# A macaron block on one core: turning h and x in the last stage with VectorE and DMAs

## The chip, the cores and the metric

The kernel runs on one core of a Trainium2 chip. The time is the device time of one execution in microseconds, the median of several runs. Engines are named as in the profile: PE (TensorE matmul) with PEld (its weight load), DVE (VectorE), ACT (ScalarE), POOL (GpSimd) and SP (SyncE), whose queue only issues DMAs here.

## The reference

x is 8192 tokens of 512 features. The block is a half-weighted small FFN, an attention block with a delta rule and a GELU MLP, and the same small FFN again:

```python
x = x + 0.5 * ffn(layernorm(x))
r = layernorm(x)
h = rmsnorm(r, ln1); r = r + gdn_attention(h)
h = rmsnorm(r, ln2); r = r + gelu(h @ w1 + b1) @ w2 + b2
x = x + r
x = x + 0.5 * ffn(layernorm(x))

# ffn(x): s = x @ Win + bin (64 columns); 16 relu terms for each column,
#         weighted by W2 and summed, + b2; then @ Wout + bout
```

Only the last stage is touched: the MLP (512 to 2048 to 512), the residuals x + r, and the second small FFN.

## The kernel before

The program has three stages behind each other. The first (to about 937 us) does the first FFN and the projections, the second (to about 1700 us) the delta rule, the third, "dense", the rest, in NT = 16 tiles of TOK = 512 tokens. A tile is Z[t % 2], 128 partitions (tokens) by 4 blocks by 512 features. Each engine has its own function with its own hand-written order (pe_dense, act_dense, dve_dense, pool_dense, sp_dense); they meet only at semaphores, and each engine works strictly in its order.

A tile has NM = 16 units m, one for each 128 of the 2048 hidden columns. In a unit PE does up(t, m), 12 matmuls (w1 against h, both split into a high and a low part, three products, lines 236 to 238 of the helper `product`), then down(t, m - 1), another 12 against w2. ACT makes gelu(t, m) (L1824) and its high part gh (L1828), DVE the low part glo (L1950). After unit 15 comes down(t, 15), and with it the tile ends on PE.

The matmuls need h with features on the partitions, while Z has tokens there. For the next tile, ACT squares z(t+1) in units 12 and 13 (L1809, sums in ss3), DVE and POOL make the inverse root (L1933, L2087), DVE scales z into the buffer H (scale_h in unit 14, L1938), and PE transposes H in 16 blocks of 128x128 into two PSUM banks (turn_h, L1683): 8 after up(t, 15) and 8 after down(t, 14). From the banks ACT writes the high part of h with the factor ln2 (h_turned, L1815) and DVE the low part (h_low, L1942).

The second small FFN of tile t - 1 runs in the units of tile t. DVE makes the statistics of the finished Z (L1960), ACT normalises it into H in units 1 and 2 (L1836), PE transposes H in units 3 and 4 (turn_x, L1692), 8 blocks each, ACT copies the banks to x2T, called xT3 in the code (x_turned, L1846). PE multiplies with Win in unit 5 (hidden, L1700), ACT and DVE do eight relus and sums in units 5 to 7 (L1854, L1980, L1984), PE multiplies with Wout in units 8 and 9 (ffn_out, L1709), DVE adds (L1990). POOL adds x1 and b2 to Z of tile t (add_x1, L2096 and L2098) once x1 has landed in H, and bout to that of tile t - 1 (L2118).

H is thus used in turn for the squares' unused output, scaled h, normalised x and x1. SP issues, for each t: load_x1(t) into H once both turns are done (L1646), the store of tile t - 1 (L1650), the load of z(t+1) into Z (L1640). The last tile's FFN is done in two halves behind the loop (turn_half and others, L1748 and L1756). In tile 0 the pieces of w2 are still being loaded and split; xT3 and Z[1] are their staging buffers, so z(1) is loaded after the last split.

## Time and profile before

| | |
|---|---|
| time, median of 3 runs | 3290.64 us (3287.76 to 3292.36) |
| the profiled execution: its time | 3292.13 us |
| its span, first to last instruction | 3290.3 us |
| mean granted clock of PE | 0.98 |
| busy: PE, PEld, DVE, ACT, POOL | 3131.8, 2549.8, 1827.6, 1405.5, 1226.3 us |
| DMA | 355.09 MB, mean 108 GB/s; HBM read 183.93 MB, written 153.09 MB |
| last stage: up and down matmuls | 6144 of 128x512, each recorded at about 0.39 us and overlapping its neighbours, so that starts are 0.23 us apart |

A line of the timeline has the start in microseconds from the span's start, the duration, the engine, the line of the code, the operation with output and input, and in brackets the idle time of the engine before it and who ended it. A matmul's recorded duration includes its way through the array, so the distance between starts is the better measure of what it costs. The chain of waits is the work that ended last, followed back from the end.

### The profile page before, as it was taken

To read this page: it belongs to the slowest core of one execution; us is meant where nothing else is said; L and a number is where in the kernel's file an instruction comes from. 1 tells how busy PE (TensorE), PEld (TensorE's weight loads), DVE (VectorE), ACT (ScalarE), POOL (GpSimd) and SP (SyncE) were. 2 spreads that over 40 slices of the span, in tenths; PEclk is the share of its full clock that TensorE was granted. 3 is DMA by queue.
4 is the path that set the end of the run, shared out by engine and by line. 5 is a ranking of instruction groups with operands and counts; after the bars stand their busy time and mean duration, and the time that the engine had idled before them with its cause. 6 is when DMAs were issued, how large, how long until landed. Compare 5 with 4: busy or idle time off the path is not lost.

```text
span 3290.3 us, 148463 instructions
## 1 busy us (share of the span) xinstructions
PE 3131.8 (95%) x68236; PEld 2549.8 (77%) x68236; DVE 1827.6 (56%) x2949; ACT 1405.5 (43%) x3166; POOL 1226.3 (37%) x1225
## 2 busy tenths in 40 slices
PE   6999999999948999999999999999999999999998
PEld 4777676767737888989888777888777888777886
DVE  6787878787748888888323333323333323333333
ACT  5544444444314554554543333433333433333433
POOL 1436565656526778766202122212122211122221
PEclk8999999999959999999999999999999999999999
DMA  3455555555466777766750110010111010111010
GB/s 114 142 148 168 155 168 143 179 142 165 137 187 188 225 223 225 216 211 199 211 155 29 39 39 26 27 39 26 39 39 35 17 39 26 39 39 39 14 39 26
DMA packets 393669, 355.09 MB, mean 108 GB/s; under 512 B 59472, under 2 KB 321744, under 8 KB 393424
## 3 DMA queue, kind: packets, MB, share of 16 engines
q1 hardware_dynamic: 391200, 350.88, 35.0%
q8 instruction: 158, 2.59, 0.3%
q10 hardware_dynamic: 2224, 0.90, 0.2%
q14 instruction: 87, 0.71, 0.1%
HBM read 183.93 MB, written 153.09 MB: 102 GB/s over the span
## 4 chain that ended last, share of the span: by engine, by line
PE 61%; DVE 7%; issue 2%; ACT 1%; DMA 0%; SPq 0%; DVEq 0%; ACTq 0%
PE bank L238 14%; PE bank L236 14%; PE bank L237 14%; PE bank L1237 8%; PE bank L1322 6%; DVE tmp L1487 2%; DVE sysf L1491 2%; PE bank L1700 2%; PE bank L1709 2%; PE bank L1692 1%; PE bank L1683 1%; DVE zb L1510 1%; DVE oT_lo L1504 1%; DVE xt L1475 1%; ACT oT_hi L1406 0%
## 5 line engine op out<-in xcount | busy, mean ns | idle before, releaser
L1950 DVE TENSOR_TENSOR glo<-gl,gh 128x512 fp32r<-128x512 f32 x256 | 196.0, 766 | 823.3 <-ACT gh L1828 821.6
L1824 ACT ACTIVATE gl<-bank,b1m 128x512 f32<-128x512 f32 x256 | 176.0, 687 | 736.1 <-PE bank L238 730.6
L236 PE MATMUL bank<-h,w_hi 128*128 128x512 f32 x1024 | 420.6, 411 | 0.1
L236 PE MATMUL bank<-w_hi,gh 128*128 128x512 f32 x1024 | 402.0, 393 | 0.8 <-DVE glo L1950 0.8
L238 PE MATMUL bank<-h,w_lo 128*128 128x512 f32 x1024 | 400.8, 391 | 0.0
L238 PE MATMUL bank<-w_hi,glo 128*128 128x512 f32 x1024 | 400.0, 391 | 0.0
L237 PE MATMUL bank<-h,w_hi 128*128 128x512 f32 x1024 | 398.8, 389 | 0.0
L237 PE MATMUL bank<-w_lo,gh 128*128 128x512 f32 x1024 | 398.6, 389 | 0.0
L1237 PE MATMUL bank<-ringA 32*32 32x32 f32 x16384 | 344.2, 197 | 10.1 <-issue 6.1
L1237 PEld LDWEIGHTS bank<-ringA 32*32 32x32 f32 x16384 | 271.9, 105 | 8.2 <-issue 2.8
L1391 ACT ACTIVATE de<-bank 128x64 f32<-128x64 f32 x512 | 114.0, 223 | 299.8 <-PE bank L1237 294.5
L237 PEld LDWEIGHTS bank<-h,w_hi 128*128 128x128 f32 x1024 | 193.2, 189 | 49.5 <-issue 10.8
L2087 POOL TENSOR_TENSOR ss<-ss,cst 128x4 f32<-128x4 f32 x15 | 15.3, 1017 | 579.7 <-DVE ss L1933 579.7
L236 PEld LDWEIGHTS bank<-h,w_hi 128*128 128x128 f32 x1024 | 192.4, 188 | 48.8 <-issue 11.3
L237 PEld LDWEIGHTS bank<-w_lo,gh 128*128 128x128 f32 x1024 | 193.3, 189 | 40.2
L238 PEld LDWEIGHTS bank<-h,w_lo 128*128 128x128 f32 x1024 | 192.2, 188 | 41.0
L238 PEld LDWEIGHTS bank<-w_hi,glo 128*128 128x128 f32 x1024 | 192.2, 188 | 40.2
L236 PEld LDWEIGHTS bank<-w_hi,gh 128*128 128x128 f32 x1024 | 192.3, 188 | 40.1 <-DVE glo L1950 1.2
L974 POOL TENSOR_TENSOR nrm<-nrm,cst 128x16 f32<-128x16 f32 x64 | 185.4, 2897 | 96.0 <-DVE nrm L768 95.3
L1491 DVE TENSOR_TENSOR sysf<-sysf,tmp 128x90 f32<-128x90 f32 (+14 forms) x210 | 198.4, 945 | 4.9
L2096 POOL TENSOR_TENSOR Z<-Z,H 128x512 f32<-128x512 f32 x64 | 92.0, 1438 | 273.4 <-DMA H<-x_scratch 273.4
L1237 PE MATMUL bank<-sT,nR 32*32 32x32 f32 x8192 | 184.2, 198 | 8.9 <-issue 8.9
(198 smaller groups left out, 7345.6 us busy)
## 6 DMA issues: line engine op xcount, KB each, us to landing
ringB<-heads_scratch SPq DMA_DIRECT2D x256, 192.0 KB, 3.3
ringA<-heads_scratch SPq DMA_DIRECT2D x256, 128.0 KB, 2.7
X<-in_L_attn_x SPq DMA_DIRECT2D x16, 1024.0 KB, 10.0
x_scratch<-X SPq DMA_DIRECT2D x16, 1024.0 KB, 4.5
heads_scratch<-vb SPq DMA_DIRECT2D x16, 1024.0 KB, 5.2
heads_scratch<-qk SPq DMA_DIRECT2D x16, 1024.0 KB, 6.9
heads_scratch<-kb SPq DMA_DIRECT2D x16, 1024.0 KB, 5.2
heads_scratch<-kbuf SPq DMA_DIRECT2D x16, 1024.0 KB, 7.1
```

What stands on the lines that cost most here:

```text
L236: e.matmul(o, lhs[0], rhs[0], start=first, stop=False)
L237: e.matmul(o, lhs[0], rhs[1], start=False, stop=False)
L238: return e.matmul(o, lhs[1], rhs[0], start=False, stop=last)
L974: e.tensor_tensor(nrm[:, u], nrm[:, u], pos_half.broadcast_to([P, TC]), ALU.pow).then_inc(o_pow, 1)
L1237: made.append(e.matmul(out[r, n, :], lhsT[r, n, :], rhs[r, n, :], start=first and n == 0, stop=True, skip_group_check=True))
L1322: m = e.matmul(bank[B_WO][:, :], oh[x][:, f, :], wo[y][:, f, :], start=k == 0, stop=k == 11)
L1391: e.activation(heads(de[c % 2][:, 2 * h:2 * h + 2, :]), bank[B_DELTA[h]][:, 0:P // 2], ACT.Copy).then_inc(a_delta[c % 4], 1)
L1487: e.tensor_tensor(tt, N[:, :, j + 1:CH, j:j + 1].broadcast_to([P, 3, rows, j]), N[:, :, j:j + 1, 0:j].broadcast_to([P, 3, rows, j]), ALU.m ...
L1491: e.tensor_tensor(N[:, :, j + 1:CH, 0:j], N[:, :, j + 1:CH, 0:j], tt, ALU.add).then_inc(v_sol, 1)
L1824: e.activation(gl[k][:, :], bank[1 - k][:, :], ACT.Gelu_apprx_tanh, bias=b1m[:, m:m + 1]).then_inc(a_gl, 1)
L1950: e.tensor_tensor(gh[k][1][:, :], gl[k][:, :], gh[k][0][:, :], ALU.subtract).then_inc(v_gl, 1)
L2096: e.tensor_tensor(z[:, b, :], z[:, b, :], H[:, b, :], ALU.add).then_inc(o_zx, 1)
```

## The change

h of tiles 1 to 15 and normalised x of tiles 0 to 14 are no longer transposed on PE. DVE turns the 32x32 blocks of H into a new buffer HT (4 instructions of 128x512), and SP then moves 16 pieces of 32 partitions by 4 by 128 numbers (64 KB each) from HT to xT3, so that features lie on partitions. Both turns use xT3. The tokens of a tile are then in the order (a, b, i) instead of (b, a, i); ACT's gelu reads its PSUM bank block by block and writes the normal order, and the relus do the same. h_turned and h_low read xT3 in SBUF instead of a PSUM bank. g3, the two relu buffers and the squares' unused output are now parts of HT.

The squares of the next tile are all made in unit 10 (before: 12 and 13), of a copy of z(t+1) that SP loads into H after x1 has been added (load_next); mean square moves to unit 11 (from 13), scale_h to 12 (from 14), with turn_h behind it. turn_x is in DVE's unit 3. Win's product, the relus and sums, Wout's product and the adds are each one unit later (6; 6, 7, 8; 9, 10). x1's load is issued by ACT in unit 5, behind the turns of x; in tile 0 it is the first that SP issues. ACT's wait for the end of stage 2 is now at its first square. The last tile's halves still turn on PE.

The diff, cut to its core:

```diff
@@ -1598,12 +1598,13 @@
             w2 = sbuf(st, "w2_hi", [P, NM, D], F32R), sbuf(st, "w2_lo", [P, NM, D], F32R)
-            g3 = sbuf(st, "g3", [P, TOK])
+            HT = sbuf(st, "HT", [P, 4 * NF, NB, 32])
             stats3 = sbuf(st, "stats3", [P, NB, 6])
             nm3 = sbuf(st, "nm3", [P, NB])
-            relu3 = [sbuf(st, f"relu3{i}", [P, TOK]) for i in range(2)]
+        work3 = HT[:, :, :, :].rearrange("p (w f) b i -> p w (f b i)", w=NB)
+        relu3, g3, junk3 = [work3[:, i, :] for i in range(2)], work3[:, 2, :], work3[:, 3, :]
         stage3 = [xT3[:, f, :] for f in range(NF)] + [Z[1][:, b, :] for b in range(NB)]
@@ -1612,12 +1613,20 @@
         HALF, LAST = TOK // 2, NT - 1
+        MOVED = 16 * 16
+        def by_block(v):
+            return v.rearrange("p (a b i) -> p b a i", a=4, b=NB)
+        def in_order(v):
+            return v.rearrange("p (b a i) -> p b a i", a=4, b=NB)
         def half(k):
-        d_H, d_w3 = sems("d_H d_w3")
+        d_H, d_w3, d_zH, d_x3, d_h3 = sems("d_H d_w3 d_zH d_x3 d_h3")
         SMALL3 = 16 * 2
...
@@ -1639,11 +1648,30 @@
-            def load_x1(t):
-                e.wait_ge(p_ht3, 4 * t + 4)
-                if t:
-                    e.wait_ge(p_xt3, 4 * t)
-                e.dma_start(H[:, :, :], x1_v[t]).then_inc(d_H, 16)
+            def load_next(t):
+                e.wait_ge(o_zx, 4 * t)
+                e.dma_start(H[:, :, :], z_v[t]).then_inc(d_zH, 16)
+            def move(landed):
+                for a4 in range(4):
+                    for q in range(4):
+                        e.dma_start(xT3[32 * q:32 * q + 32, :, a4 * P:(a4 + 1) * P],
+                                    HT[32 * a4:32 * a4 + 32, q:4 * NF:4, :, :].rearrange("j f b i -> j f (b i)"),
+                                    ).then_inc(landed, 16)
+            def move_x(t):
+                e.wait_ge(v_tx, 4 * t + 4)
+                e.wait_ge(a_hi3, 4 * t + 8)
+                e.wait_ge(v_lo3, 4 * t + 8)
+                move(d_x3)
+            def move_h(t):
+                e.wait_ge(v_th, 4 * t)
+                if t >= 2:
+                    e.wait_ge(p_win, NT + t - 1)
+                else:
+                    e.wait_ge(v_wlo3, 12)
+                move(d_h3)
             def store(t):
@@ -1653,14 +1681,20 @@
+            e.wait_ge(p_ht3, 4)
+            e.dma_start(H[:, :, :], x1_v[0]).then_inc(d_H, 16)
             for i in range(8, NP3):
             for t in range(NT):
-                load_x1(t)
+                if t:
+                    move_x(t - 1)
+                if t + 1 < NT:
+                    load_next(t + 1)
                 if t:
                 if t + 1 < NT:
+                    move_h(t + 1)
                     load_z(t + 1)
@@ -1675,26 +1709,8 @@
-            def turn_h(t, f):
-                bk = 6 + f % 2
-                e.wait_ge(v_hs, 4 * t + 4)
-                bank_free(bk)
-                for b in range(NB):
-                    m = e.transpose(bank[bk][:, b * P:(b + 1) * P], H[:, b, f * P:(f + 1) * P], ident)
-                m.then_inc(p_ht3, 1)
-                released[bk] = v_lo3, 4 * t + f + 1
-            def turn_x(t, f):
-                bk = 6 + f % 2
-                e.wait_ge(a_y3, 4 * t + 4)
-                bank_free(bk)
-                for b in range(NB):
-                    m = e.transpose(bank[bk][:, b * P:(b + 1) * P], H[:, b, f * P:(f + 1) * P], ident)
-                m.then_inc(p_xt3, 1)
-                released[bk] = a_xT3, 4 * t + f + 1
             def hidden(t):
-                e.wait_ge(a_xT3, 4 * t + 4)
+                e.wait_ge(d_x3, MOVED * (t + 1))
                 bank_free(6)
...
@@ -1765,30 +1781,21 @@
             def ffn(t, m):
-                if m in (3, 4):
-                    turn_x(t, 2 * (m - 3))
-                    turn_x(t, 2 * (m - 3) + 1)
-                elif m == 5:
+                if m == 6:
                     hidden(t)
-                elif m in (8, 9):
-                    ffn_out(t, 2 * (m - 8))
-                    ffn_out(t, 2 * (m - 8) + 1)
+                elif m in (9, 10):
+                    ffn_out(t, 2 * (m - 9))
+                    ffn_out(t, 2 * (m - 9) + 1)
                     up(t, m)
-                    if m == NM - 1 and t + 1 < NT:
-                        turn_h(t + 1, 0)
-                        turn_h(t + 1, 1)
                     if m:
                         ffn(t - 1, m)
-                if t + 1 < NT:
-                    turn_h(t + 1, 2)
-                    turn_h(t + 1, 3)
                 down(t, NM - 1)
@@ -1798,21 +1805,27 @@
         def act_dense(e):
+            def load_x1(t):
+                e.wait_ge(v_tx, 4 * t)
+                e.dma_start(H[:, :, :], x1_v[t]).then_inc(d_H, 16)
             def square(t, b):
                 if b == 0:
-                    e.wait_ge(d_x[t % 2], 16 * ((NT + t) // 2 + 1))
-                    if t:
-                        e.wait_ge(v_hs, 4 * t)
-                        e.wait_ge(o_zx, 4 * t)
-                    if t >= 2:
-                        e.wait_ge(p_xt3, 4 * (t - 1))
-                e.activation(H[:, b, :], Z[t % 2][:, b, :], ACT.Square, accum_out=ss3[:, b:b + 1]).then_inc(a_ss, 1)
+                    e.wait_ge(d_zH, 16 * t)
+                    e.wait_ge(v_hs, 4 * t)
+                    if t == 1:
+                        e.wait_ge(done2, 5)
+                else:
+                    e.wait_ge(a_ss, 4 * t + b)
+                e.activation(junk3, H[:, b, :], ACT.Square, accum_out=ss3[:, b:b + 1]).then_inc(a_ss, 1)
             def h_turned(t, f):
-                e.wait_ge(p_ht3, 4 * t + f + 1)
                 if f == 0:
+                    e.wait_ge(d_h3, MOVED * t)
                     e.wait_ge(p_up, NM * t)
-                e.activation(hT3[0][:, f, :], bank[6 + f % 2][:, :], ACT.Copy, scale=ln2[:, f:f + 1]).then_inc(a_hi3, 1)
+                e.activation(hT3[0][:, f, :], xT3[:, f, :], ACT.Copy,
+                             scale=ln2[:, f:f + 1]).then_inc(a_hi3, 1)
             def gelu(t, m):
@@ -1821,7 +1834,10 @@
                     e.wait_ge(d_w3, SMALL3)
-                e.activation(gl[k][:, :], bank[1 - k][:, :], ACT.Gelu_apprx_tanh, bias=b1m[:, m:m + 1]).then_inc(a_gl, 1)
+                made, ordered = bank[1 - k][:, :], gl[k][:, :]
+                if t:
+                    made, ordered = by_block(made), in_order(ordered)
+                e.activation(ordered, made, ACT.Gelu_apprx_tanh, bias=b1m[:, m:m + 1]).then_inc(a_gl, 1)
                 e.wait_ge(a_gl, n + 1)
@@ -1830,20 +1846,9 @@
             def normalize(t, b):
                     e.wait_ge(v_nm3, t + 1)
-                    if t + 1 < NT:
-                        e.wait_ge(p_ht3, 4 * (t + 1) + 4)
-                    e.wait_ge(o_zx, 4 * t + 4)
+                    e.wait_ge(v_th, 4 * t + 4)
                 e.activation(H[:, b, :], Z[t % 2][:, b, :], ACT.Identity, bias=nm3[:, b:b + 1],
                              scale=rs3[:, b:b + 1]).then_inc(a_y3, 1)
-            def x_turned(t, f):
-                e.wait_ge(p_xt3, 4 * t + f + 1)
-                if f == 0:
-                    if t:
-                        e.wait_ge(p_win, NT + t)
-                    else:
-                        e.wait_ge(v_wlo3, NP3)
-                e.activation(xT3[:, f, :], bank[6 + f % 2][:, :], ACT.Copy).then_inc(a_xT3, 1)
             def relus(t, *hs):
...
@@ -1912,9 +1912,11 @@
                         ffn(t - 1, m)
-                    if t + 1 < NT and m in (12, 13):
-                        square(t + 1, 2 * (m - 12))
-                        square(t + 1, 2 * (m - 12) + 1)
+                    if t and m == 5:
+                        load_x1(t)
+                    if t + 1 < NT and m == 10:
+                        for b in range(NB):
+                            square(t + 1, b)
                 if t + 1 < NT:
@@ -1935,11 +1937,28 @@
             def scale_h(t):
                 for b in range(NB):
-                    e.tensor_scalar(H[:, b, :], Z[t % 2][:, b, :], ss3[:, b:b + 1], None, ALU.mult).then_inc(v_hs, 1)
+                    e.tensor_scalar(H[:, b, :], H[:, b, :], ss3[:, b:b + 1], None, ALU.mult).then_inc(v_hs, 1)
+            def turn(b):
+                return e.transpose(HT[:, :, b, :], H[:, b, :])
+            def turn_h(t):
+                if t >= 2:
+                    e.wait_ge(p_wout, 4 * (NT + t - 1))
+                for b in range(NB):
+                    e.wait_ge(v_hs, 4 * t + b + 1)
+                    turn(b).then_inc(v_th, 1)
+            def turn_x(t):
+                if t:
+                    e.wait_ge(d_h3, MOVED * (t + 1))
+                for b in range(NB):
+                    e.wait_ge(a_y3, 4 * t + b + 1)
+                    turn(b).then_inc(v_tx, 1)
             def h_low(t, f):
                 e.wait_ge(a_hi3, 4 * t + f + 1)
-                e.scalar_tensor_tensor(hT3[1][:, f, :], bank[6 + f % 2][:, :], ln2[:, f:f + 1], hT3[0][:, f, :],
+                e.scalar_tensor_tensor(hT3[1][:, f, :], xT3[:, f, :], ln2[:, f:f + 1], hT3[0][:, f, :],
                                        ALU.mult, ALU.subtract).then_inc(v_lo3, 1)
             def gelu_low(t, m):
...
@@ -2031,15 +2050,17 @@
                     shift(t)
-                elif m == 5:
+                elif m == 3:
+                    turn_x(t)
+                elif m == 6:
                     sums(t, 0, 1)
-                elif m == 6:
+                elif m == 7:
                     sums(t, 2, 3, 4)
-                elif m == 7:
+                elif m == 8:
                     sums(t, 5, 6, 7)
-                elif m in (8, 9):
-                    add_ffn(t, 2 * (m - 8))
-                    add_ffn(t, 2 * (m - 8) + 1)
+                elif m in (9, 10):
+                    add_ffn(t, 2 * (m - 9))
+                    add_ffn(t, 2 * (m - 9) + 1)
@@ -2056,10 +2077,11 @@
                         ffn(t - 1, m)
-                    if t + 1 < NT and m == 13:
+                    if t + 1 < NT and m == 11:
                         mean_square(t + 1)
-                    if t + 1 < NT and m == 14:
+                    if t + 1 < NT and m == 12:
                         scale_h(t + 1)
+                        turn_h(t + 1)
                 if t + 1 < NT:
@@ -2090,9 +2112,11 @@
                     e.wait_ge(d_H, 16 * (t + 1))
-                    e.wait_ge(v_hs, 4 * t + 4)
                     if t == 0:
+                        e.wait_ge(v_hs, 4)
                         e.wait_ge(d_w3, SMALL3)
+                    else:
+                        e.wait_ge(d_x[t % 2], 16 * ((NT + t) // 2 + 1))
                 e.tensor_tensor(z[:, b, :], z[:, b, :], H[:, b, :], ALU.add).then_inc(o_zx, 1)
```

## Rows read from the trace of the kernel before

**Rows 1.** the page, its head and part 1: busy time, share, instructions.

```profile
span 3290.3 us, 148463 instructions
...
PE 3131.8 (95%) x68236; PEld 2549.8 (77%) x68236; DVE 1827.6 (56%) x2949; ACT 1405.5 (43%) x3166; POOL 1226.3 (37%) x1225
```

**Rows 2.** windows: length, busy (count) PE, PEld, DVE, ACT, POOL; clock, DMA, GB/s.

```profile
1800.00:1897.87 97.87, 97.87 (x434) 78.52 (x433) 33.80 (x51) 36.70 (x60) 19.40 (x15) 1.00 0.10 33
...
1893.70:3166.20 1272.50, 1272.50 (x5618) 1020.97 (x5618) 442.04 (x651) 477.06 (x780) 253.11 (x195) 1.00 0.10 33
```

**Rows 3.** chain of waits, 2395 to 2500, shares of it by line.

```profile
by line: PE bank L238 30.3%; PE bank L237 30.1%; PE bank L236 29.9%; PE bank L1700 3.3%; PE bank L1709 3.3%; PE bank L1692 1.7%; PE bank L1683 1.7%
```

**Rows 4.** timeline (start, us, engine, line): PE transposes, then two gelus.

```profile
2402.00 1.03 PE L1692 MATMUL bank<-cst,H 128*128 128x128 f32 x8
...
2408.36 1.03 PE L1692 MATMUL bank<-cst,H 128*128 128x128 f32 x8
...
2457.35 0.69 ACT L1824 ACTIVATE gl<-bank,b1m 128x512 f32<-128x512 f32 x1 [4.11 <-PE bank L238]
...
2462.81 0.69 ACT L1824 ACTIVATE gl<-bank,b1m 128x512 f32<-128x512 f32 x1 [2.88 <-PE bank L238]
```

**Rows 5.** first tile: SP timeline; PE waits (total, times, longest).

```profile
1773.84 0.38 SPq L1640 DMA_DIRECT2D Z<-z_scratch  x1
...
PE bank L236 <- DVE glo L1950: 0.8, 1, 0.8
```

**Rows 6.** timeline of DVE and ACT, tile end; squares, by line.

```profile
2464.20 0.69 DVE L1950 TENSOR_TENSOR glo<-gl,gh 128x512 fp32r<-128x512 f32 x1 [4.77 <-ACT gh L1828]
...
2470.27 1.67 DVE L1938 TENSOR_SCALAR H<-Z,ss 128x512 f32<-128x512 f32 x4
...
2475.72 1.41 DVE L1942 SCALAR_TENSOR_TENSOR h<-bank,ln,h 128x512 fp32r<-128x512 f32 x2
...
2474.98 1.25 ACT L1815 ACTIVATE h<-bank,ln 128x512 fp32r<-128x512 f32 x2
...
L1809 ACT ACTIVATE H<-Z 128x512 f32<-128x512 f32 x60 | 36.9, 618 | 6.4 <-DMA Z<-z_scratch 6.4
```

**Rows 7.** groups by line, DVE: busy us, mean ns of one, idle before.

```profile
L757 DVE STREAM_TRANSPOSE vb<-proj 128x512 f32<-128x512 f32 x64 | 44.5, 696 | 32.1 <-ACT proj L536 32.1
```

**Rows 8.** L1145: issue ns min/median/max, landing; SP timeline around one.

```profile
L1145 SPq DMA_DIRECT2D ringA<-xt x224: 470/471/943, 1061.6 to 1686.2; - x112
...
DMA to landing us min/median/max: 1.9/3.0/4.5
...
1508.00 0.47 SPq L1145 DMA_DIRECT2D ringA<-xt  x1
...
1508.55 0.56 SPq L1154 DMA_DIRECT2D ringB<-heads_scratch  x1
```

**Rows 9.** POOL's timeline in one tile; DMA issues (KB each, median us to landing).

```profile
2415.03 1.26 POOL L2096 TENSOR_TENSOR Z<-Z,H 128x512 f32<-128x512 f32 x1 [15.93 <-DMA H<-x_scratch]
...
2425.17 1.62 POOL L2098 TENSOR_TENSOR Z<-Z,b2b 128x512 f32<-128x512 f32 x1
...
2465.68 1.02 POOL L2087 TENSOR_TENSOR ss<-ss,cst 128x4 f32<-128x4 f32 x1 [38.89 <-DVE ss L1933]
...
H<-x_scratch SPq DMA_DIRECT2D x16, 1024.0 KB, 5.5
```

**Rows 10.** three DMAs of L283 in SP's timeline, landing of two, line L286's issues.

```profile
136.58 1.64 SPq L283 DMA_DIRECT2D lt_scratch<-ltb  x3
...
lt_scratch<-ltb SPq DMA_DIRECT2D x16, 384.0 KB, 3.9
...
lt_scratch<-ltb SPq DMA_DIRECT2D x16, 128.0 KB, 4.8
...
L286 SPq DMA_DIRECT2D heads_scratch<-pb x48: 472/1364/2796, 138.3 to 936.3; - x48
```

**Rows 11.** line L1984 on DVE: ns min/median/max.

```profile
L1984 DVE SCALAR_TENSOR_TENSOR g<-relu,w2t,g x105: 742/753/1784, 1833.3 to 3213.5; 128x512 f32<-128x512 f32 x105
```

More of the change, by code:

```diff
@@ L1626, in macaron @@
             "a_whi3 a_ss a_hi3 a_xT3 a_gl a_gh a_y3 a_relu3")
-        v_wlo3, v_ms, v_hs, v_lo3, v_gl, v_x2, v_bn3, v_ag3, v_nm3, v_g3, v_o = sems(
-            "v_wlo3 v_ms v_hs v_lo3 v_gl v_x2 v_bn3 v_ag3 v_nm3 v_g3 v_o")
+        v_wlo3, v_ms, v_hs, v_lo3, v_gl, v_x2, v_bn3, v_ag3, v_nm3, v_g3, v_o, v_tx, v_th = sems(
+            "v_wlo3 v_ms v_hs v_lo3 v_gl v_x2 v_bn3 v_ag3 v_nm3 v_g3 v_o v_tx v_th")
         o_ms, o_zx, o_sb, o_rs3, o_xb3 = sems("o_ms o_zx o_sb o_rs3 o_xb3")
@@ L1749, in turn_half @@
                     m.then_inc(p_xt3, 1)
-                    released[bk] = a_xT3, 4 * LAST + 2 * k + n + 1
+                    released[bk] = a_xT3, 2 * k + n + 1
             def hidden_half(k):
-                e.wait_ge(a_xT3, 4 * LAST + 2 * k + 2)
+                e.wait_ge(a_xT3, 2 * k + 2)
                 bank_free(k)
@@ L1853, in relus @@
                         e.wait_ge(v_g3, 8 * t + h - 1)
-                    e.activation(relu3[h % 2][:, :], bank[6][:, :], ACT.Relu, bias=b1t[:, h:h + 1],
+                    e.activation(in_order(relu3[h % 2]), by_block(bank[6][:, :]), ACT.Relu, bias=b1t[:, h:h + 1],
                                  scale=w1t[:, h:h + 1]).then_inc(a_relu3, 1)
@@ L1865, in turned_half @@
                 for n in range(2):
-                    e.wait_ge(p_xt3, 4 * LAST + 2 * k + n + 1)
+                    e.wait_ge(p_xt3, 2 * k + n + 1)
                     if k == 0 and n == 0:
                         e.wait_ge(p_win, NT + LAST)
+                        e.wait_ge(v_lo3, 4 * NT)
                     e.activation(xT3[:, 2 * n:2 * n + 2, half(k)],
@@ L1891, in ffn @@
                     normalize(t, 3)
-                elif m in (3, 4):
-                    x_turned(t, 2 * (m - 3))
-                    x_turned(t, 2 * (m - 3) + 1)
-                elif m == 5:
+                elif m == 6:
                     relus(t, 0, 1)
-                elif m == 6:
+                elif m == 7:
                     relus(t, 2, 3, 4)
-                elif m == 7:
+                elif m == 8:
                     relus(t, 5, 6, 7)
             for t in range(NT):
-                if t == 1:
-                    e.wait_ge(done2, 5)
                 for m in range(NM):
@@ L1979, in sums @@
                             e.wait_ge(p_wout, 4 * (NT + t))
-                        e.tensor_scalar(g3[:, :], relu3[0][:, :], w2t[:, 0:1], b2t[:, 0:1],
+                        e.tensor_scalar(g3, relu3[0], w2t[:, 0:1], b2t[:, 0:1],
                                         ALU.mult, ALU.add).then_inc(v_g3, 1)
@@ L1983, in sums @@
                         e.wait_ge(v_g3, 8 * t + h)
-                        e.scalar_tensor_tensor(g3[:, :], relu3[h % 2][:, :], w2t[:, h:h + 1], g3[:, :],
+                        e.scalar_tensor_tensor(g3, relu3[h % 2], w2t[:, h:h + 1], g3,
                                                ALU.mult, ALU.add).then_inc(v_g3, 1)
@@ L2033, in ffn @@
                     shift(t)
-                elif m == 5:
+                elif m == 3:
+                    turn_x(t)
+                elif m == 6:
                     sums(t, 0, 1)
-                elif m == 6:
+                elif m == 7:
                     sums(t, 2, 3, 4)
-                elif m == 7:
+                elif m == 8:
                     sums(t, 5, 6, 7)
-                elif m in (8, 9):
-                    add_ffn(t, 2 * (m - 8))
-                    add_ffn(t, 2 * (m - 8) + 1)
+                elif m in (9, 10):
+                    add_ffn(t, 2 * (m - 9))
+                    add_ffn(t, 2 * (m - 9) + 1)
             for i in range(AHEAD3):
```

## The prediction

> **What bounds the kernel now.** I read the page first. The profiled execution has a span of 3290.3 us and its own time is 3292.13 us, so 1.8 us lie around the span; PE is busy 95% of it, DVE 56%, ACT 43% [rows 1]. Then the table by windows: in the last stage one tile of 512 tokens repeats with a period of 97.87 us, 13 periods make 1272.5 us, PE is busy in all of it and the granted clock is 1.00, its upper level of 2.4 GHz [rows 2]. The reader is to see that PE never waits there, so every microsecond of PE work taken away is one gained, as long as what replaces it arrives on time. The chain of waits over one period says the same: it holds nothing but matmuls, 1.7% of 105 us each for the transposes at L1692 and L1683 [rows 3]. ACT, DVE and POOL are busy 36.7, 33.8 and 19.4 us of a period and the DMA engines a tenth of it [rows 2]: there is room for new work, and only its latency can hurt.
>
> **The change part by part.**
>
> *The transposes go.* Per tile PE ran four batches of 8 (two for h, two for x). A unit of up and down is 5.46 us, by two gelus in a quiet stretch; with a batch in it, from batch to batch, it is 8 transposes more and 6.36 us [rows 4]. So a batch costs 0.90 us; the chain's share, two batches of a line in 1.79 us, gives 0.89 for either line [rows 3]. There are 15 tiles with turned h and 15 with turned x: 30 x 2 x 0.90 = 54.0 us, all on the path. With 0.89 it is 53.4. The last tile's own turns stay on PE.
>
> *The wait in the first tile goes.* In tile 0 the squares waited for Z, whose load was issued only at 1773.84, after the last split of w2; gelu of unit 13 was queued behind them on ACT, and PE lost 0.8 us [rows 5]. After the change the squares read a copy of z in H, loaded as soon as x1 has been added, so this goes. Nothing else is late there: 0.8 us gained.
>
> *What must now arrive on time: h.* I count from E12, the end of up(12). The tile ends 4 units after it, at E12 + 21.8 (up(15) ends at +16.4, then down(14) and down(15)). Before, gelu to the end of glo took 2.1 us (gelu at 2462.81, glo from 2464.20 for 0.69) and four scalings 1.7 [rows 4, 6]. The new DVE turns are the same instruction as L757, 128x512 f32 with blocks of 32 written 128 apart, 0.70 each [rows 7]: four are 2.8, ready at 2.1 + 1.7 + 2.8 = 6.6. The inputs are there: four squares of 0.62 at m = 10 [rows 6] and POOL's root of 1.0 [rows 9], two units earlier. SP then issues 16 DMAs of 64 KB, 128 runs of 512 B each. The nearest row is L1145, SBUF to SBUF, 64 KB: 0.47 of issue, the next DMA starts 0.55 after it, and landing takes 3.0 in the median, 4.5 at most [rows 8]. First issue 6.7, last 6.7 + 15 x 0.55 = 14.9, landed 17.9. ACT is through with gelu(15) at 16.4 + 1.4 = 17.8, so h_turned starts at once: 0.63 for hi, 0.70 for lo [rows 6], first lo at about 19.4, wanted at 21.8; the following pieces come each 0.70 and are used each 0.68. h may land as late as 20.4: 2.5 us of slack.
>
> *What must arrive on time: x.* From E3: glo done 2.1, four turns 2.8, first issue 5.0, last 13.2, landed 16.2. hidden is now after down(5), at 3 x 5.46 + 2.73 = 19.1: the later unit is what makes room, and costs nothing itself, as the out-projections and adds only shift by 5.5 us in a tile with 30 us free behind them. Slack 2.9 us. x1's load of 1 MB is issued by ACT at E5 + 1.4 = E3 + 12.3, beside the last two or three moves. It alone takes 5.5 us [rows 9]; I let it cost the moves nothing to 1.5 us, still hidden.
>
> *The two bounds of the move.* The row above has 128 partitions; the new DMAs have 32 on both sides, for which no row has this size. The best bound upward is the last of three DMAs at L283, 32 partitions and 128 KB: the three are issued in 1.64 us, some 0.55 apart, the one before lands after 3.9 and the last after 4.8 [rows 10]. That is 0.55 + 4.8 - 3.9 = 1.45 us more for 128 KB, 0.72 for 64 KB, if the data and not the issue sets the pace. Below, 64 KB at the issue's 0.47 is the least. With a pace of s per DMA h is late from 6.7 + 15s + 3.0 > 20.4, s > 0.71, and x from 5.0 + 15s + 3.0 > 19.1, s > 0.74. I take 0.55, from the nearest row: nothing is late. At 0.72 h is 0.1 late and x fits by 0.3, but then x1's load runs into the last third of the moves and may make them later.
>
> The Trainium skill, DMA: Bandwidth & Descriptors, section Bandwidth, speaks against the change: it wants 1 MiB per DMA and calls transfers under 64 KB descriptor-dominated. The trace shows what this case can pay: a 64 KB DMA lands 3.0 us after issue, but the next is issued 0.55 later [rows 8], so the fixed part overlaps. By the rule read as one fixed cost after the other the change would lose; by the row it is hidden.
>
> *Queues passed and waits added.* SP waits for v_th before move_h; behind it is only Z's load for the next tile, issued at about E12 + 15.5 and landed some 6 us later, wanted by POOL when x1 lands, 35 us into the next tile. POOL's eight adds took 11.8 us from there (2415.03 to 2425.17 + 1.62) [rows 9], over at 47 of 94; they meet the sums on DVE as before. Their end releases z's second load into H (about 5.6 us), landed at 53, before the squares at E10 + 1.4 = 61. ACT's load_x1 waits for v_tx, true at E3 + 4.9 and reached at E3 + 12.3: no wait; its issue delays gelu(6) by nothing, 4 us are free. The square's fourfold serial waits end before gelu(11). The extra z traffic and the moves, 3 MB a tile, raise the DMA share from 0.10 to about 0.2.
>
> *Work on ACT and DVE.* The four copies x2T fall away, the 8 turns (5.6 us) and DMA traffic come in: neither engine is the bound. Gelu and relu now read PSUM in runs of 32. No row shows that on PSUM; the tight place is glo(15), now wanted 2.73 us after up(15) and ready after 2.1, as it was for m = 0 all along. If gelu were twice as slow, 0.1 us twice a tile would be lost, 2 us in all; I take 0. h_low reads two SBUF operands where one was in PSUM. At L1984, which does, it takes 0.753 in the median and up to 1.784 [rows 11]; 0.753 is in the slack, and and at the tile's end POOL is not adding (its last work there is the root) [rows 9]. The Trainium skill, SBUF — State Buffer, Door 1, says that non-contiguous PSUM access slows matmuls; these reads are ACT's, in runs of 128 B, and no run here shows it, so it changes neither sum nor chance.
>
> *Sum.* 54.0 + 0.8 = 54.8 us. Profiled time 3292.13 - 54.8 = 3237.3; against the median of the three runs, 3290.64, 1.5 below the profiled one, 3235.8. I forecast 3236 us. The period becomes 97.87 - 3.6 = 94.27.
>
> **The rivals.**
>
> (a) *The moves land slightly late, faster still.* Pace 0.72 and x1's load sharing the DMA engines: at E3 + 12.3 six moves are outstanding, and at half speed they need some 3 us more, landing at 5.0 + 10.8 + 3.0 + 3 = 21.8 against 19.1. With h's 0.1, 2.8 x 15 = 42 us are given back: 3236 + 42 = 3278. Without the sharing, paces from 0.72 to 0.85 cover 3238 to 3291. For it: 32 partitions in the row that gives 0.72. Against: that transfer left for HBM behind 896 KB of others.
>
> (b) *The moves are slow: slower than before.* One mechanism: SP issues each small strided DMA at the cost of L286, whose median is 1.36 us [rows 10]. The place is h at the tile's end and x before hidden. h is late by 6.7 + 20.4 + 3.0 - 20.4 = 9.7 and x by 5.0 + 20.4 + 3.0 - 19.1 = 9.3, less 3.6: 15.4 a tile, 231 us in all, 3467. It decides from 30s = 25.4 on, s = 0.85 (both delays together eat 3.64). Against: L286 has 256 to 1024 runs in a DMA, here 128, and it stood behind a full megabyte; the plain 64 KB row has 0.47. At 1.0 it would be 3236 + 15 x (4.3 + 3.9) = 3359, slower too.
>
> A last one: the 16 DMAs run one after the other, each for its whole 3.0 us. Then a move takes 48 us, h is late by 6.7 + 48 - 20.4 = 34 and x by 5.0 + 48 - 19.1 = 34, and the time is 3236 + 15 x 68 = 4256. The next issue 0.55 later speaks against it, with landings that overlap; 1 in 100. This is what the Trainium skill's rule named above (DMA: Bandwidth & Descriptors, Bandwidth) would come to here.
>
> (c) *Nothing is gained.* The transposes are hidden already, or the period is set elsewhere. Chain and windows exclude it nearly; only a chance meeting of late moves and gain (s near 0.85) gives 3284 to 3297.
>
> **How the numbers follow.** Forecast 0.70 (3231 to 3240), (a) 0.14 (3240 to 3284), (c) 0.03 (within 0.2%, which is 6.6 us and about what a measurement of this kernel can tell from no change), (b) 0.12 and the serial case 0.01. The range goes from 3231 to 3278: it holds the forecast and three quarters of (a), 0.80. Low end: the forecast less 5, the spread of the runs before (3287.76 to 3292.36). Faster by over 0.2% 0.84, same 0.03, slower 0.13.
>
> **What the profile after would show.** A period of 94.3 by windows, with PE busy in all of it. L1683 and L1692 gone from the chain. 480 SP issues of H's turned copy to x2T, 0.5 to 0.55 apart. ACT h_turned right behind gelu(15), or an idle before it that ends with a DMA: that much is the delay minus 2.5. A wait of PE at L1700 on a DMA to x2T would be x's. 60 + 60 new stream transposes of 0.70. Gelu at 0.69 still. The prediction is wrong if the pace per move is over 0.71, if landing takes over 5.5 us after the last issue, or if gelu grows beyond 1.3 us.

## The result and the profile after

| | before | after |
|---|---|---|
| time, median | 3290.69 us (3287.76 to 3292.36) | 3241.03 us (3238.52 to 3252.07) |
| ratio, 95% interval | | 0.9857 [0.9845, 0.9868] |
| profiled execution: time, span | 3292.13, 3290.3 us | 3238.52, 3236.7 us |
| last stage, from its first up-matmul to the end | 1585.0 us | 1539.4 us |
| its period, in a quiet tile | 97.87 us | 94.3 us |

The change saves 49.7 us, 1.5%; the forecast was 54.8 us and 3236 us. The page of the kernel after, its head and part 1, beside [rows 1]:

```profile
span 3236.7 us, 147953 instructions
...
PE 3080.1 (95%) x67756; PEld 2497.4 (77%) x67756; DVE 1880.3 (58%) x3069; ACT 1381.5 (43%) x3106; POOL 1225.6 (38%) x1225
```

The spans differ by 53.6 us, but 8.0 of that lie ahead of the changed code: the last stage began at 1697.3 us and not at 1705.3. In its two profiled runs the changed kernel began it at 1697.3 and 1701.6, and in the other kernels of this study it came between 1700.4 and 1709.9, with the same code before it. So I compare the last stage alone, where 45.6 us are gained. The tile loop of that stage and the last tile's halves behind it can be told apart too. Up to its last up- or down-matmul the loop took 1556.4 us before and 1510.9 after, the rest 28.6 and 28.5 us. One period by windows, beside [rows 2] (length, busy time and count of PE, PEld, DVE, ACT, POOL, then clock, DMA share, GB/s):

```profile
2295.00:2389.30 94.30, 94.30 (x402) 75.16 (x401) 37.89 (x58) 35.03 (x56) 19.15 (x16) 1.00 0.25 67
```

In this quiet tile PE is busy throughout, the period is the forecast's 94.3 (over all tiles the products with Win are 94.9 us apart in the mean), DVE has 38 instead of 34 us of work and the DMA share is 0.25 instead of 0.10. But not every tile is quiet. PE's waits in the last stage (total, times, longest):

```profile
PE bank L1716 <- DMA x2T<-HT: 6.6, 10, 1.6
```

L1716 is the product with Win, the line that was L1700 [rows 3]. It waited for a move of x in 10 of 15 tiles. By the starts of its matmuls it came late in the other five too, by at most 0.4 us. From the last matmul ahead of a product to the first behind it 3.27 us pass undisturbed; here it is 9.9 us more in all 15 together. The chain of waits shows the longest one (start, us, what):

```profile
2468.26 0.58 SPq L1658
...
2475.32 0.60 SPq L1658
2475.97 1.25 SPq L1658
...
2478.65 5.75 DMA x2T<-HT
...
2484.44 3.70 PE bank L1716 x8
```

The line at 2468.26 is the first of 16 issues of a move, each 0.60 us with a start every 0.64, but for two of 1.25 and 0.71. The last landed 5.75 us after its issue, where the median of all 480 moves is 2.1. Then the product takes 3.70 us and not 3.43, at a granted clock of 1.00 (window 2484.4 to 2488.2): behind such a wait its first matmul no longer overlaps the one before and is recorded at 0.70 instead of 0.59 us. The same tile's h, and ACT's issue of x1's load (timeline; ACTq is ACT's DMA queue):

```profile
2429.13 2.48 DVE L1943 STREAM_TRANSPOSE HT<-H 128x512 f32<-128x512 f32 x4
...
2431.64 10.68 SPq L1658 DMA_DIRECT2D x2T<-HT  x16
...
2443.80 2.56 ACT L1827 ACTIVATE h<-x2T,ln 128x512 fp32r<-128x512 f32 x4 [0.52 <-DMA x2T<-HT]
...
2475.40 0.37 ACTq L1810 DMA_DIRECT2D H<-x_scratch  x1
```

ACT's issue did not slow SP's. It lay inside the SP issue at 2475.32, which took its 0.60 us, and was over before the one of 1.25 began. Of the 18 SP issues that overlapped an issue of x1's load in this profile 16 took 0.60, and of the nine single moves that took over 1 us to issue four belong to h, where ACT issues nothing. The moves of h in one tile (ns min/median/max of the 16 issues):

```profile
L1658 SPq DMA_DIRECT2D x2T<-HT x16: 591/602/1786, 2623.1 to 2633.9; - x16
```

What makes a few issues long stays open.

The groups by line, beside [rows 6, 7, 11] (busy us, mean ns of one, idle before):

```profile
L1840 ACT ACTIVATE gl<-bank,b1m 128x512 f32<-128x512 f32 x256 | 176.7, 690 | 785.4 <-PE bank L238 785.4
...
L1943 DVE STREAM_TRANSPOSE HT<-H 128x512 f32<-128x512 f32 x120 | 74.5, 678 | 0.0
...
L1961 DVE SCALAR_TENSOR_TENSOR h<-x2T,ln,h 128x512 fp32r<-128x512 f32 x60 | 41.1, 746 | 7.8 <-ACT h L1827 7.3
...
L2003 DVE SCALAR_TENSOR_TENSOR HT<-HT,w2t 128x512 f32<-128x512 f32 x105 | 106.9, 1019 | 8.2 <-DVE HT L2003 0.5
```

Gelu's strided read of PSUM costs nothing (690 against 687 ns), DVE's turns are 0.68 each, and h_low with two operands in SBUF is 746 against 745 ns. L2003 is the old L1984, with the same median (752 and 753 ns) and a lower mean (1.02 us instead of 1.14). Of its 105 instructions 30 are long, before it was 45, and in both profiles each of the long ones, and none of the short, overlaps work of POOL.

### The profile page after: what moved, and what is told of

It is laid out like the page before. It is cut to its first block, busy times and chain, and to the rows that moved or that the text cites. A ratio compares the mean times of both kernels' runs of the same rounds, so it can differ in the third digit from the quotient of the medians.

```text
span 3236.7 us, 147953 instructions
## 1 busy us (share of the span) xinstructions
PE 3080.1 (95%) x67756; PEld 2497.4 (77%) x67756; DVE 1880.3 (58%) x3069; ACT 1381.5 (43%) x3106; POOL 1225.6 (38%) x1225
## 4 chain that ended last, share of the span: by engine, by line
PE 55%; DVE 8%; SPq 3%; issue 2%; DMA 2%; ACT 1%; DVEq 0%; ACTq 0%
PE bank L238 12%; PE bank L236 12%; PE bank L237 12%; PE bank L1237 9%; PE bank L1322 6%; SPq L1658 3%; DVE tmp L1487 2%; DVE sysf L1491 2%; DMA x2T<-HT 2%; PE bank L1716 2%; PE bank L1725 2%; DVE zb L1510 1%; DVE HT L1943 1%; DVE oT_lo L1504 1%; ACT oT_hi L1406 0%
## 5 line engine op out<-in xcount | busy, mean ns | idle before, releaser
L1237 PE MATMUL bank<-de,ringB 32*32 32x32 f32 x8192 | 184.6, 197 | 5.1 <-ACT de L1391 4.4
```

Of the source, the lines that this page charges most:

```text
L1237: made.append(e.matmul(out[r, n, :], lhsT[r, n, :], rhs[r, n, :], start=first and n == 0, stop=True, skip_group_check=True))
```

## The experiments

All ran beside the kernel before; "the stage" is the last stage as in the table. The base is the changed kernel, run again.

**The changed kernel again.** No edit.

> The changed kernel once more, as the base for the three runs beside it. Theory A (the PE transposes are gone at 0.90 us a batch, and the moves of x land up to 2 us late for the product with Win, which costs 6.6 us of PE waits and some 2.6 us of slower restarts in the last stage): the same as before, about 3240 us, with a PE wait at L1716 of 4 to 9 us in all. Rival B (the missing 5 us against the forecast are only scatter of the first two stages): the wait at L1716 is there but the time of the last stage from its first up-matmul to the end is under 1535 us.

Measured: 3242.45 us, ratio 0.9855 [0.984, 0.987]; the stage 1538.7 us, PE's wait at L1716 4.5 us. So the stage repeats within 1 us, and it is over 1535: what is missing of the forecast's 54.8 us is missing in the stage, not in the scatter ahead of it.

**x turned in unit 2.** DVE's order alone:

```diff
-                elif m == 3:
+                elif m == 2:
                     turn_x(t)
```

> One edit against the changed kernel: VectorE turns x at the end of unit 2, behind the second half of the normalisation, and not in unit 3. Theory A: HT is ready some 4.5 us earlier, so the last move lands before x1's load starts and well before the product with Win; the PE wait at L1716 goes to 0, the first matmuls of the product are back at 3.43 us, and the time falls by 7 to 10 us against the changed kernel. Rival B: no change beyond 2 us, as the wait was covered by something else. Rival C (the moves are late because SP issues them slowly, whatever the start): they still take 0.64 us each, but 4.5 us of earlier start is more than the longest wait of 2.0, so C gives the same time as A; the two are told apart by the run beside it in which x1 loads later.

Measured: 3234.54 us, ratio 0.9832 [0.9818, 0.9846]; the stage 1529.8 us, no wait at L1716. The chain of this kernel has the product at its undisturbed length:

```profile
2485.84 3.43 PE bank L1716 x8
```

7.9 us less in the median, 8.9 in the stage than in the base: theory A's number. All five times (3232.15 to 3239.88 us) are under the base's lowest, 3241.67, though the first measurement of the changed kernel had one of 3238.52. 54.8 us off 1585.0 would be 1530.2; the forecast's sum for the PE side was right.

The loop alone repeats better than the stage. It is 1501.1 us here and in the three others without a wait at the product (x1's load in unit 6, both early, eight moves of 128 KB). Their stages differ by 1.9 us, and this lies in the last tile's halves behind the loop: 28.7 us here and 26.8 to 26.9 in the other three, with a granted clock of 0.76 and 0.81 over that stretch.

**x1's load in unit 6.** ACT's order alone:

```diff
+                    if t and m == 6:
+                        load_x1(t)
                     if t:
                         ffn(t - 1, m)
-                    if t and m == 5:
-                        load_x1(t)
```

> One edit against the changed kernel: x1's load is issued by ScalarE in unit 6 and not in unit 5, so it can't share the DMA engines with the moves of x. Theory A (x1's load stretches the landing of the last moves from about 2.1 to 4.6 to 5.8 us): landing falls to about 2 to 2.5 us, the wait at L1716 goes to 0, time 7 to 10 us less, as in the run beside it. Rival C (pace of issue alone): the wait stays at 6 us and the time within 2 us. GpSimd's adds end 5.5 us later in both; that should still be in time for the squares of unit 10, if not PE waits there by up to 1 us a tile, 15 us in all.

Measured: 3235.97 us, ratio 0.9834 [0.9821, 0.9848]; the stage 1527.9 us, no wait at L1716. First two lines of the kernel after, then this kernel's product and load (KB each, median us to landing):

```profile
x2T<-HT SPq DMA_DIRECT2D x480, 64.0 KB, 2.1
...
H<-x_scratch ACTq DMA_DIRECT2D x15, 1024.0 KB, 6.5
```

```profile
2488.42 3.43 PE bank L1716 x8
...
H<-x_scratch ACTq DMA_DIRECT2D x15, 1024.0 KB, 5.5
```

The moves start when they did in the changed kernel and are issued at the same pace, and yet x is in time; x1's load is itself faster, 5.5 for 6.5 us. In the tile shown SP even needed 11.1 us to the last issue, one of them 2.0 us long. So it is x1's load beside them that made the last moves late, and the slow issue alone would have been hidden. Rival C falls. The adds that end 5.5 us later cost nothing.

**PE's transposes put back, for nobody.** 32 a tile, into a free bank:

```diff
+            def idle_turns(t):
+                bank_free(7)
+                for b in range(8):
+                    c = slice(b % 4 * P, (b % 4 + 1) * P)
+                    e.transpose(bank[7][:, c], wout[:, c], ident)
...
+                if m in (3, 4):
+                    idle_turns(t)
...
+                    if m == NM - 1 and t + 1 < NT:
+                        idle_turns(t + 1)
...
+                if t + 1 < NT:
+                    idle_turns(t + 1)
```

> Against the changed kernel: PE makes again four batches of 8 transposes of 128x128 for each of 15 tiles, at the old places, from a constant into a free PSUM bank, and nobody waits for them; all else is as changed. Theory A: 60 batches at 0.90 us are 54 us more, and as the product with Win comes 1.8 us later behind two of them, the wait at L1716 (6.6 us and slower restarts) almost goes: 3241 + 54 - 8 = about 3287, within 4 us of the kernel before. Rival D (part of the gain comes from ScalarE and VectorE, relieved of reading PSUM, or from the first tile): the time is 3270 to 3280, clearly under the kernel before.

Measured: 3290.67 us, ratio 0.9997 [0.9988, 1.0006]; the stage 1584.6 us, no wait of PE at the product. Two of the batches in its chain (in this kernel L1716 is the added transposes, the product is L1722):

```profile
2477.52 0.87 PE bank L1716 x8
...
2503.92 0.87 PE bank L1716 x8
```

The loop takes 1556.0 us, 54.9 more than the 1501.1 without them and without a wait: 0.91 us for each of the 60 batches. Before it was 1556.4. So but for 0.4 us the gain is PE's instructions, and no more than that can be relief of ACT or DVE or the first tile's wait. Against the changed kernel the stage is 1584.6 - 1538.7 = 45.9 us longer: the transposes add 54.9, and their 1.8 us ahead of the product take the waits away.

**The small FFN in its old units.** On PE, ACT and DVE each unit number one less; x1's load stays behind gelu of unit 5, and so is now ahead of the relus (on PE:)

```diff
-                if m == 6:
+                if m == 5:
                     hidden(t)
-                elif m in (9, 10):
+                elif m in (8, 9):
...
```

> Against the changed kernel the small FFN is back in its old units on all engines: product with Win in unit 5, relus and sums in 5 to 7, product with Wout and adds in 8 and 9; x1's load stays right behind gelu of unit 5. Theory A: the moves of x land 19.6 to 20.7 us after E3 (the end of up(3)) and the product is wanted at E3 + 13.65 instead of 19.1, so PE waits about 6 us at L1716 in each of 15 tiles, 90 us and some 4 us of slower restarts: about 3325 us, slower than the kernel before. Rival B: the later unit was no more than a precaution, within 10 us of the changed kernel.

Measured: 3355.95 us, ratio 1.0209 [1.0192, 1.0226]; the stage 1649.9 us. Its wait, the product in the chain, and windows of one tile ahead of the wait, in the product and behind it:

```profile
PE bank L1716 <- DMA x2T<-HT: 85.6, 15, 6.4
...
2437.57 5.87 PE bank L1716 x8
...
2420.00:2430.00 10.00, 10.00 (x46) 8.26 (x45) 3.68 (x6) 1.90 (x3) 0.00 (x0) 1.00 0.31 59
...
2436.00:2440.00 4.00, 2.43 (x3) 1.17 (x4) 0.00 (x0) 0.00 (x0) 3.32 (x3) 0.50 0.13 22
...
2440.00:2450.00 10.00, 10.00 (x36) 6.78 (x35) 5.37 (x5) 4.89 (x7) 6.82 (x6) 0.90 0.32 97
```

The wait is 85.6 us in 15 tiles, as expected. The time is 30 us over the expectation, for a reason that I had not seen: after a wait of 5.5 us the granted clock is 0.50, the 1.2 GHz level, and the product takes 5.87 us for 3.43. With this for all 15, 85.6 + 15 x 2.44 = 122.2, and the stage is 121.9 us longer than the 1528 of the kernels that don't wait. All 15 products took 5.58 us or more. In the changed kernel's profile the waits are at most 1.6 us and the product takes 3.70. In its second profile the longest wait, 1.9 us, is in the last tile, and there it is 5.40, while its other 14 are at 3.43 to 3.70; the chain and the window of that product:

```profile
3151.60 5.40 PE bank L1716 x8
...
3151.60:3157.00 5.40, 5.40 (x9) 2.36 (x10) 0.00 (x0) 0.00 (x0) 5.24 (x5) 0.68 0.00 0
```

So the lower clock came into the changed kernel too, in one tile of one of its two profiles.

**Both: FFN in its old units and x turned in unit 2.** The two edits above together.

> As the run beside it, FFN in its old units, and in addition VectorE turns x in unit 2. Theory A: the first move is issued at E3 + 0.1, the last of 16 lands 10.3 + 2.1 us later, at E3 + 12.5, before x1's load starts and 1.1 us before the product is wanted: no wait at L1716, about 3234 us, the same as with the turn in unit 2 alone. Then it is the landing against its deadline alone that decides, and the unit's delay could be had for nothing either way. If landing needs over 13.5, PE waits that excess in each tile: each us costs 15.

Measured: 3234.32 us, ratio 0.9841 [0.9825, 0.9858]; the stage 1528.0 us, no wait at L1716. SP's timeline, one move of x:

```profile
2466.31 10.25 SPq L1658 DMA_DIRECT2D x2T<-HT  x16
```

So the later unit and the earlier turn are two ways to the same slack, and either costs nothing; the earlier turn is enough alone, the later unit falls 9.8 us short. Without both the change loses 2%; with the later unit alone it gains 1.4 to 1.5% (the changed kernel's two measurements), with the earlier turn alone 1.6, with both 1.7.

**Eight more DMAs ahead of h.**

```diff
+                for n in range(2):
+                    for q in range(4):
+                        e.dma_start(xt_d[4 * n:4 * n + 4, 32 * q:32 * q + 32, :, :].rearrange("f j n i -> j f (n i)"),
+                                    HT[32 * n:32 * n + 32, q:4 * NF:4, :, :].rearrange("j f b i -> j f (b i)"),
+                                    ).then_inc(d_h3, 16)
                 move(d_h3)
...
```

> Against the changed kernel SP issues 8 more DMAs of 64 KB of the same shape ahead of each move of h, from HT to a scratch in HBM that nobody reads. Theory A (h has a slack of its own): they take 8 x 0.64 = 5.1 us of SP; in the trace of the changed kernel h had 1.7 us of slack between landing and the first up-matmul, so PE waits about 3.4 us in each of 15 tiles, 51 us, with restarts 55: about 3295 us. Rival B (what matters is only the moves' landing for x): no change from 3241. Rival C (the forecast's slack of 2.5 us): 2.6 a tile, 3281.

Measured: 3283.9 us, ratio 0.9983 [0.9974, 0.9993]; the stage 1577.4 us. SP's timeline, and PE's wait at the first up-matmul:

```profile
2460.88 3.73 SPq L1676 DMA_DIRECT2D xt_scratch<-HT  x8
...
2464.65 10.25 SPq L1658 DMA_DIRECT2D x2T<-HT  x16
...
PE bank L236 <- DVE h L1966: 28.1, 15, 2.8
```

The eight took 3.77 us and not 5.1, since to HBM a start comes every 0.47. PE waited 1.9 us a tile in the mean, so h's slack had been 3.77 - 1.9 = 1.9 us, near theory A's 1.7; with waits from 1.3 to 2.8 us it lies between 1.0 and 2.4, under the forecast's 2.5 in every tile. The median, near rival C's, comes from the cheaper DMAs, not from a larger slack. The stage grew by 38.7 us, 2.6 a tile. Much of the 0.7 beyond the recorded wait is the clock, here behind waits shorter than in the run above. Of the seven waits of 2.1 us and more five were followed, at once or within 1.3 us, by a granted clock of 0.50, of the eight shorter ones none. Two windows right behind a wait, of 2.8 and of 1.4 us:

```profile
2771.90:2775.10 3.20, 3.18 (x8) 2.50 (x9) 3.20 (x6) 1.02 (x2) 0.00 (x0) 0.50 0.60 231
...
2477.95:2481.00 3.05, 3.05 (x13) 2.46 (x14) 3.05 (x6) 0.99 (x2) 0.00 (x0) 1.00 0.70 267
```

In the first, matmuls start 0.43 us apart and not 0.23; eight of them cost 1.6 us more. Five times this is 8 us of the stage, by my estimate. Rival B falls: h has its own point from which it decides.

**The same 64 KB over 128 partitions.**

```diff
-                        e.dma_start(xT3[32 * q:32 * q + 32, :, a4 * P:(a4 + 1) * P],
-                                    HT[32 * a4:32 * a4 + 32, q:4 * NF:4, :, :].rearrange("j f b i -> j f (b i)"),
+                        e.dma_start(xT3[:, q, a4 * P:(a4 + 1) * P],
+                                    HT[:, 4 * q + a4, :, :].rearrange("j b i -> j (b i)"),
```

> Against the changed kernel each of the 16 moves keeps its 64 KB and its runs of 512 B, but takes one run from each of 128 partitions and not four from each of 32; the numbers land in wrong places, so only the time is meant. Theory A (the shape makes SP's issue 0.60 instead of the 0.47 of the row from before): issue falls to about 0.47, a start every 0.52, the last move of x starts 1.9 us earlier, the wait at L1716 falls from 4 to 7 us to under 1 us and the time to about 3235. Rival B: issue stays at 0.60, no change in time; then SBUF as destination, or the queue, sets the pace.

Measured: 3234.8 us, ratio 0.9837 [0.982, 0.9853]; the stage 1532.4 us. The line's issues (ns min/median/max) and PE's wait:

```profile
L1658 SPq DMA_DIRECT2D x2T<-HT x480: 464/601/2075, 1774.2 to 3141.9; - x160
...
PE bank L1716 <- DMA x2T<-HT: 1.8, 2, 1.3
```

Neither theory holds whole. The issue stays at 0.60 in the median, only the first of a move is at 0.46, so the 32 partitions did not slow it. But the wait fell to 1.8 us, so over 128 partitions the last moves stand x1's load better: a move lands 1.9 us after its issue in the median instead of 2.1, and the last of a move of x 3.5 to 4.8 us after it instead of 4.4 to 5.8. Why is open.

**Eight moves of 128 KB.**

```diff
-        MOVED = 16 * 16
+        MOVED = 8 * 16
...
-                    for q in range(4):
-                        e.dma_start(xT3[32 * q:32 * q + 32, :, a4 * P:(a4 + 1) * P],
-                                    HT[32 * a4:32 * a4 + 32, q:4 * NF:4, :, :].rearrange("j f b i -> j f (b i)"),
+                    for q in range(2):
+                        e.dma_start(xT3[:, 2 * q:2 * q + 2, a4 * P:(a4 + 1) * P],
+                                    HT[:, 8 * q + a4:8 * q + a4 + 5:4, :, :].rearrange("j f b i -> j f (b i)"),
```

> Against the changed kernel each move is 8 DMAs of 128 KB, two runs of 512 B for each of 128 partitions, in place of 16 of 64 KB; the same 1 MB and as many runs, the numbers land in wrong places, so only the time is meant. In the traces so far a start comes every 0.64 us with 32 or with 128 partitions. Theory A (each issue has its fixed price, whatever it moves): a start every 0.64 us, a move of h or x is issued in 5.1 us, x lands about 5 us earlier than in the changed kernel, before x1's load, no wait at L1716, about 3234 us. Theory B (the 0.64 is 64 KB at about 100 GB/s, the data sets the pace and the issue waits for it): a start every 1.28 us after the first few, the move takes 10 us as before, the wait at L1716 stays between 1.8 and 6.6 us, 3235 to 3242 us.

Measured: 3232.96 us, ratio 0.9827 [0.981, 0.9843]; the stage 1528.0 us. A move in SP's timeline, and the line's issues:

```profile
2433.73 5.25 SPq L1658 DMA_DIRECT2D x2T<-HT  x8
...
L1658 SPq DMA_DIRECT2D x2T<-HT x240: 593/621/1713, 1774.5 to 3134.8; - x120
```

Eight issues take 5.25 us, 0.66 each, landing 2.2 in the median: up to 128 KB the price is per DMA, not per byte. Theory A. This shape is not the real permutation, in which each piece goes from 32 partitions to 32 others; whether that can be had in eight DMAs no run shows.

## Why the prediction was right, point by point

The path, the cost of the transposes and the question that decides were right; the answer for x was not. The median of 3241.03 us lies in the range, but 1 us above the forecast's own band (3231 to 3240) and so in that of rival (a). A sign that the prediction had named for being wrong, a landing over 5.5 us after the last issue, did come, in two tiles (5.75 and 5.6). And that the profiled executions differ by 53.6 us, so close to 54.8, is luck: 8.0 us of it is scatter ahead of the stage.

**What bounds.** PE, without a wait: confirmed by the transposes put back, 3290.67 against 3290.64 us of the kernel before.

**The transposes, 54.0 us, and the first tile, 0.8.** Confirmed by the stage of the five kernels without or almost without a wait at the product (1527.9 to 1532.4, forecast 1530.2), and closer by the loop, 1556.4 - 1501.1 = 55.3 us. By the transposes put back it is 0.91 us a batch, and 0.4 us is left for the first tile, where no wait remains.

**h in time.** The forecast had the first issue at E12 + 6.7, landing at 17.9. In the traced tile (E12 = 2425.5) it was 6.1 and 18.3. Two terms were off and cancelled: a start every 0.64 and not 0.55, which is 1.4 us over 15 starts, and a landing of 2.1 and not 3.0. By the same sum that leaves 20.4 - 18.3 = 2.1 us in this tile; over all tiles the eight added DMAs gave 1.9, forecast 2.5.

**x in time: the term that was mis-sized.** The sum had first issue at E3 + 5.0, last landing at 16.2, deadline 19.1, and allowed x1's load 0 to 1.5 us. In the worst tile (E3 = 2463.7) it was 4.6 and 20.7, 4.5 us later: the first issue - 0.4, the pace 15 x 0.09 = + 1.4, the two long SP issues + 0.7, and a landing of 5.75 for 3.0, + 2.8. So what the sum had too small is the pace and, above all, the landing beside x1's load: 5.75 us where it had 3.0 and 0 to 1.5 for the load. That is rival (a)'s mechanism, in its place, at about a quarter of its size. The stage is 11.4 us longer than the 1528.0 of the kernels that don't wait: 6.6 are waits and 3.4 the slower products behind them (11 at 3.70 for 3.43 and four between), and the rest lies behind the loop, where the last tile's halves took 28.5 us and not 26.8 (granted clock 0.75 and 0.81). The loop alone is 1510.9 - 1501.1 = 9.8 us longer. In the second profile the stage is 10.7 longer: 4.5 of waits and 4.9 of products, 2.0 of them in the one of 5.40. (a) had 42. The two runs, with the load later and with the turn earlier, show the cause from both sides. The price in the median is 3241 to 3242 against 3234.5, 7 us.

**The bound from the 32-partition row, 0.72.** The pace was 0.64, between the ends, but not for the reason weighed: neither the partitions nor the bytes set it, but the issue.

**Rival (b)** took the 3.6 us of gain off twice. 3236 us already has them, so at 1.36 us per DMA it is 3236 + 15 x 19.0 = 3521 and not 3467, as its own line for a pace of 1.0 does it; its place, its threshold of 0.85 and the chances don't rest on that. Its mechanism is the one the FFN in its old units shows: a delay beyond the slack goes to the period one to one, and more where it brings the lower clock. It did not happen because a DMA of 64 KB costs 0.64 and not 0.85 or more. The Trainium skill's preference for 1 MiB (DMA: Bandwidth & Descriptors, section Bandwidth) came to this here: 16 DMAs of 64 KB cost 10.3 us of issue, eight of 128 KB 5.25, and the fixed part of landing overlapped. Here the rule names the right direction, and the deadline decides whether it matters.

**Contention of h_low with POOL.** None of the 60 h_low overlapped work of POOL, and they took 746 ns. Of the sums (L2003, two inputs in SBUF) the 30 that overlapped it were long, up to 1.79 us, the other 75 stayed at about 0.75. The Trainium skill, SBUF — State Buffer, section Who interferes with whom, says that a VectorE instruction with two SBUF inputs contends with a GpSimd instruction that reads SBUF; the trace agrees in both cases.

**Best version.** The changed kernel with x turned in unit 2: 3234.5 us, faster than both (ratio 0.9832 to the kernel before). With the FFN in its old units as well it is the same, 3234.3.

## What to carry to other kernels

Where TensorE never waits, work taken from it is gained in full (here 55.3 us of the forecast's 54.8), and the question is only whether what replaces it lands before its deadline: count from a fixed event to the last landing and compare with the wanted time, for each move. A chain of many small DMAs is priced per issue, and a big load that starts within its last pieces delays exactly the piece that is awaited: start it after the landing, or the chain a unit earlier. A wait of TensorE can cost twice, in the wait and in a slower clock behind it: here never after up to 1.7 us, in six of eight cases after 1.9 to 2.8, and always after 5.2 or more.

## What the runs showed of the hardware

- SBUF to SBUF, one after the other on SP: 0.60 us of issue and a start every 0.64 to 0.66, the same for 64 KB on 32 partitions, 64 KB on 128 and 128 KB on 128. To HBM, with the same source, 0.47. The row of before that I used (0.47, and 0.55 to the next) stood alone between loads.
- An issue of ACT beside them changed nothing: 16 of the 18 SP issues that overlapped one took 0.60 us. A few issues took over 1 us, up to 2.1, with and without it.
- Landing of such a move is 2.0 to 2.1 us alone (up to 3.4 next to a long issue) and up to 7.1 beside a load of 1 MB, which itself goes from 5.5 to 6.5.
- After 5.46 us without work TensorE's granted clock was 0.50 (from 2436 to 2440) and the 8 records of a product took 5.87 us. After waits up to 1.6 us they took 3.70 at a granted clock of 1.00, after one of 1.9 us 5.40 at 0.68, undisturbed 3.43. With eight more DMAs ahead of h, five of seven waits of 2.1 to 2.8 us were followed by 0.50.
- A VectorE instruction with two inputs in SBUF: 0.75 us alone, up to 1.79 over work of GpSimd.
- ScalarE reading a PSUM bank in runs of 32 numbers: 690 against 687 ns.
